# A mixture-of-experts front: statistics taken earlier, another split of the norm, sums before the low half, first tile prepared ahead

## The reference, cut to what matters

```python
x = x + tanh(g_xattn[1]) * L1_xattn(layernorm(x), ctx, mask, ...)
x = x + tanh(g_ffn[1]) * L1_ffn(layernorm(x), ...)

def L1_ffn(hidden, norm_weight, router_w, sw1, sb1, sw2, sb2, ew1, eb1, ew2, eb2):
    var = mean(square(hidden), axis=-1, keepdims=True)
    normed = hidden * rsqrt(var + 1e-08) * norm_weight
    shared = maximum(normed @ sw1 + sb1, 0.0) @ sw2 + sb2
    probs = sigmoid(flat @ router_w.T)              # 8 experts
    scores, idx = top_k(probs, 2)
    w = scores / (sum(scores, axis=-1, keepdims=True) + 1e-06)
    h = maximum(einsum('td,edh->teh', flat, ew1) + eb1[None], 0.0)
    eo = einsum('teh,eho->teo', h, ew2) + eb2[None]
    return shared + einsum('teo,te->to', eo, comb)  # comb holds w at idx
```

## Time and profile before

| | us |
|---|---|
| median of 3 runs | 1716.51 |
| lowest, highest | 1713.88, 1717.43 |
| the profiled execution's own time | 1717.06 |
| its span, from first to last instruction | 1715.3 |
| TensorE busy | 1420.7 (83%) |
| VectorE busy | 1235.3 (72%) |
| ScalarE busy | 1116.1 (65%) |
| GpSimd busy | 214.6 (13%) |
| mean granted TensorE clock | 0.917 |

### The profile page before, as it was taken

How to read it: one execution, slowest core, us unless ns; L and a number is a source line. 1 busy time by engine, 2 the same in 40 slices (tenths; PEclk the granted TensorE clock), 3 DMA queues, 4 the chain that set the end, 5 groups by cost and what they waited for, 6 DMA issues and landing times. The chain is left out here.

```text
span 1715.3 us, 40917 instructions
## 1 busy us (share of the span) xinstructions
PE 1420.7 (83%) x15436; PEld 1010.6 (59%) x15436; DVE 1235.3 (72%) x3086; ACT 1116.1 (65%) x2453; POOL 214.6 (13%) x189
## 2 busy tenths in 40 slices
PE   1799999999999992680638898989889588899996
PEld 1467666766666762440625566566666366678884
DVE  6478888788788777678656898989888675334443
ACT  5467777777777763375236888888888452356663
POOL 4400000001000001200041000000000000034443
PEclk9999999999999997795857999999999588999998
DMA  4123232233222211000021121211100162112221
GB/s 143 52 69 109 83 96 90 81 105 95 97 93 93 72 56 56 1 0 0 1 78 40 49 82 42 82 42 33 33 17 11 32 226 63 47 30 45 48 49 23
DMA packets 64912, 105.72 MB, mean 62 GB/s; under 512 B 7433, under 2 KB 38898, under 8 KB 63570
## 3 DMA queue, kind: packets, MB, share of 16 engines
q1 hardware_dynamic: 58002, 94.83, 17.5%
q0 software_dynamic: 6720, 8.27, 2.9%
HBM read 68.88 MB, written 35.11 MB: 61 GB/s over the span
## 5 line engine op out<-in xcount | busy, mean ns | idle before, releaser
L1272 ACT ACTIVATE a_p<-a_s,a_nb 112x375 f32<-112x375 f32 x256 | 140.9, 598 | 26.2 <-DVE a_nb L1373 25.3
L294 PE MATMUL a_ps_o<-a_vh,a_pt 125*128 125x64 f16 (+1 forms) x1536 | 153.2, 183 | 3.0 <-ACT a_pt L1285 0.8
L1197 PE MATMUL a_ps_t<-ident,a_p 112*128 112x112 f32 x768 | 119.4, 288 | 40.0 <-ACT a_p L1272 39.5
L296 PE MATMUL a_ps_o<-a_vh,a_pt 125*128 125x64 f16 (+1 forms) x1536 | 151.3, 182 | 0.0
L295 PE MATMUL a_ps_o<-a_vl,a_pt 125*128 125x64 f16 (+1 forms) x1536 | 151.2, 182 | 0.0
L584 ACT ACTIVATE a_pt<-a_ps_t 125x336 f16<-125x336 f32 x256 | 102.7, 448 | 68.6 <-PE a_ps_t L515 68.0
L576 ACT ACTIVATE a_p<-a_ps_s,a_nb 112x375 f32<-112x375 f32 x256 | 143.8, 573 | 3.3 <-DVE a_scaled L667 3.3
L294 PEld LDWEIGHTS a_ps_o<-a_vh,a_pt 125*128 125x128 f16 x1536 | 133.8, 98 | 15.7 <-ACT a_pt L1285 7.4
L1364 DVE TENSOR_TENSOR a_s<-a_ps_s,a_mask 112x750 f32<-112x750 f32 x128 | 119.8, 936 | 26.2 <-PE a_ps_s L1187 21.1
L295 PEld LDWEIGHTS a_ps_o<-a_vl,a_pt 125*128 125x128 f16 x1536 | 131.2, 98 | 11.3
L1197 PEld LDWEIGHTS a_ps_t<-ident,a_p 112*128 112x128 f32 x768 | 81.4, 148 | 94.6 <-issue 80.1
(11 more groups left out here) (360 smaller groups left out, 4553.7 us busy)
## 6 DMA issues: line engine op xcount, KB each, us to landing
a_piece<-in_w SPq DMA_DIRECT2D x72, 256.0 KB, 3.1
split_weights<-a_pair SPq DMA_DIRECT2D x72, 256.0 KB, 3.4
w<-split_weights SPq DMA_DIRECT2D x8, 1024.0 KB, 6.1
a_ctx<-in_ctxT SPq DMA_DIRECT2D x16, 375.0 KB, 3.6
ctx<-a_cx SPq DMA_DIRECT2D x16, 375.0 KB, 4.3
a_cx<-ctx SPq DMA_DIRECT2D x16, 375.0 KB, 5.2
w1h<-split_weights SPq DMA_DIRECT2D x2, 1792.0 KB, 14.0
w1l<-split_weights SPq DMA_DIRECT2D x2, 1792.0 KB, 16.6
```

Source lines behind the costliest of these rows:

```text
L294: nc.tensor.matmul(out, wh, mh, start=(i == 0), stop=False)
L296: last = nc.tensor.matmul(out, wl, mh, start=False, stop=(i == n - 1))
L1197: mm = nc.tensor.matmul(ps_t[:, 2 * (g % 2) + i, t * S:(t + 1) * S], p32[:, g % 2, i, t * KV:t * KV + 128], ident32[0:S, 0:S], start=(t == ...
L1272: nc.scalar.activation(p32[:, g % 2, i, 0:NC], s2[:, g % 2, i, :], ACT.Exp, bias=nb[:, g % 2, i:i + 1], scale=-1.0).then_inc(exp_done, 1)
```

## The change

It has four parts.

1. The 16 `bn_stats` leave the front. VectorE issues them in the last slots of the second attention: five in each of the slots 128, 129 and 130, and the last one behind the last `W`. `stats` becomes a buffer that both phases see.
2. VectorE norms the blocks 0 to 11 group by group, with `low_x` of the group before behind each group of norms; the splits of the router's weights and of the biases move behind `low_x(0)`. ScalarE does the square roots first, then norms the blocks 12 to 15, then makes its small copies, and only then `high_x`. TensorE transposes two groups before the first `up`.
3. In a step, VectorE's `add` stands before `low`.
4. The register loads of the expert numbers, the transposition of tile 0 and its split move to the end of the front, in the buffers `tile_xh`, `tile_xl` that both phases see. The routed experts start with the first layer of tile 0.

```diff
@@ attention1_phase, VectorE
                     low(name, b)
                 if 0 <= g - 2 < G and (g - 2) % NP == NP - 1:
                     normalise((g - 2) // NP)
+                if g == G:
+                    dve.wait_ge(job_lo, NUMBER["W", B - 2] + 1)
+                if G <= g < G + 3:
+                    for t in range(5 * (g - G), 5 * (g - G) + 5):
+                        nc.vector.bn_stats(stats[:, t, :], x_res[:, t, :])
+            dve.wait_ge(job_lo, NUMBER["W", B - 1] + 1)
+            nc.vector.bn_stats(stats[:, B - 1, :], x_res[:, B - 1, :])
@@ moe_front_phase, SyncE
-                if g < NG // 2:
+                if g < NG - 1:
                     sp.wait_ge(normed, TG * (g + 1))
                 else:
-                    sp.wait_ge(normed_act, TG * (g + 1 - NG // 2))
+                    sp.wait_ge(normed_act, TG)
@@ moe_front_phase, TensorE
             for g in range(NG):
                 transpose(g)
-                if g < NG - 1:
-                    up(g)
+                if g > 0:
+                    up(g - 1)
             route()
...
                 if n == FIND_AT:
                     find()
+            pe.wait_ge(experts_ready, 1)
+            for n in range(NPACK):
+                experts.append(pe.snap(pe.value_load(tile_expert[0:1, n:n + 1], min_val=0, max_val=8 ** PACK - 1)))
+            pe.wait_ge(xt_in[0], 16)
+            pe.wait_ge(index_ready, 1)
+            for k in range(KD):
+                mm = nc.tensor.transpose(px[:, 0, k * 128:(k + 1) * 128], xt32[:, 0, k * 128:(k + 1) * 128], ident32[:])
+            mm.then_inc(tile_transposed, 1)
@@ moe_front_phase, ScalarE
+            act.wait_ge(var_ready, 1)
+            nc.scalar.activation(small[:, 1, :], small[:, 0, :], ACT.Sqrt).then_inc(std_ready, 1)
+            act.wait_ge(var_ready, 2)
+            nc.scalar.activation(small[:, 4, :], small[:, 3, :], ACT.Sqrt).then_inc(std_ready, 1)
+            act.wait_ge(scale_ready, 1)
+            act.wait_ge(kept, 16 * B)
+            for t in range(B - TG, B):
+                nc.scalar.activation(norm[:, t, 0:D], norm[:, t, 0:D], ACT.Identity, bias=small[:, 7, t:t + 1],
+                                     scale=small[:, 6, t:t + 1]).then_inc(normed_act, 1)
             act.wait_ge(small_in, NSMALL)
...
-            for t in range(HALF, B):
-                nc.scalar.activation(norm[:, t, 0:D], norm[:, t, 0:D], ACT.Identity, bias=small[:, 7, t:t + 1],
-                                     scale=small[:, 6, t:t + 1]).then_inc(normed_act, 1)
-                if t % 4 == 3:
-                    high_x(t // 4 - 2)
+            high_x(0)
+            high_x(1)
+            hidden(0)
             high_x(2)
-            hidden(0)
+            hidden(1)
             high_x(3)
-            hidden(1)
...
+            act.wait_ge(tile_transposed, 1)
+            nc.scalar.activation(xth[:, 0, :], px[:, 0, 0:D], ACT.Copy).then_inc(tile_hi, 1)
@@ moe_front_phase, VectorE
-            for t in range(B):
-                last = nc.vector.bn_stats(stats[:, t, :], norm[:, t, 0:D])
             stat(last)
...
-            for t in range(HALF):
-                nc.vector.tensor_scalar(norm[:, t, 0:D], norm[:, t, 0:D], mv[:, t, 0:1], small[:, 6, t:t + 1],
-                                        ALU.subtract, ALU.mult).then_inc(normed, 1)
-            low_x(0)
-            low_x(1)
+            for g in range(NG - 1):
+                for t in range(g * TG, g * TG + TG):
+                    nc.vector.tensor_scalar(norm[:, t, 0:D], norm[:, t, 0:D], mv[:, t, 0:1], small[:, 6, t:t + 1],
+                                            ALU.subtract, ALU.mult).then_inc(normed, 1)
+                if g > 0:
+                    low_x(g - 1)
+                if g == 1:
+                    dve.wait_ge(nw_ready, 1)
+                    dve.wait_ge(rw_hi, KD)
...
+                    dve.wait_ge(b2_hi, 1)
+                    nc.vector.scalar_tensor_tensor(out=b2[:, 1], in0=b2_32, scalar=WS, in1=b2[:, 0], op0=ALU.mult,
+                                                   op1=ALU.subtract).then_inc(b2_ready, 1)
...
             for n in range(10, STEPS + LAG + 1):
+                if n % HC1 == LAG and n > LAG:
+                    add(n // HC1 - 1)
                 if n < STEPS:
                     low(n)
-                if n % HC1 == LAG and n > LAG:
-                    add(n // HC1 - 1)
...
+            dve.wait_ge(tile_hi, 1)
+            nc.vector.tensor_tensor(xtl[:, 0, :], px[:, 0, 0:D], xth[:, 0, :], ALU.subtract).then_inc(tile_lo, 1)
@@ routed_experts_phase
-            experts = [pe.snap(pe.value_load(tile_expert[0:1, n:n + 1], min_val=0, max_val=8 ** PACK - 1))
-                       for n in range(NPACK)]
...
             expert(0)
-            transpose(0)
...
-            split_x(0)
```

More of the change, by code:

```diff
@@ L1467, in moe_front_phase @@
          rows_out, numbered, shared_in, w1_in, up_done, relu_done,
-         h_hi, h_lo, down_done, bias_chain, added, gate_made) = (sem(f"m_{n}") for n in names)
+         h_hi, h_lo, down_done, bias_chain, added, gate_made, experts_ready) = (sem(f"m_{n}") for n in names)
         y_in = [sem(f"m_y_in{i}") for i in range(2)]
+        experts, xth, xtl, tile_transposed, tile_hi, tile_lo = first_tile
         NSMALL = 16 * 4
@@ L1767, in _ @@
             nc.vector.tensor_scalar(var, mv[:, :, 1], 1e-5, None, ALU.add).then_inc(var_ready, 1)
-            dve.wait_ge(nw_ready, 1)
-            dve.wait_ge(rw_hi, KD)
-            for k in range(KD):
-                last = nc.vector.scalar_tensor_tensor(out=rw[:, k, 1, :], in0=rw32[:, k, :], scalar=nws[:, k:k + 1],
-                                                      in1=rw[:, k, 0, :], op0=ALU.mult, op1=ALU.subtract)
-            last.then_inc(rw_ready, 1)
             reciprocal_root(var, std, rstd, 1)
@@ L1940, in routed_experts_phase @@
         y, half = sb("e_y", [128, YR, D]), sb("e_half", [128, 2, D])
+        p2 = ps("e_p2", [128, 2, 512])
+        p1 = ps("e_p1", [128, 4, 512])
         px = ps("e_px", [128, 2, 512])
-        p1 = ps("e_p1", [128, 4, 512])
-        p2 = ps("e_p2", [128, 2, 512])
-        names = ("x_transposed", "x_hi", "x_lo", "up_done", "relu_done", "h_hi", "h_lo", "down_done", "half_ready",
-                 "y_ready", "y_out")
-        (x_transposed, x_hi, x_lo, up_done, relu_done, h_hi, h_lo, down_done, half_ready, y_ready,
-         y_out) = (sem(f"e_{n}") for n in names)
+        experts, xth, xtl, x_transposed, x_hi, x_lo = first_tile
+        names = ("up_done", "relu_done", "h_hi", "h_lo", "down_done", "half_ready", "y_ready", "y_out")
+        (up_done, relu_done, h_hi, h_lo, down_done, half_ready, y_ready, y_out) = (sem(f"e_{n}") for n in names)
         block = ctx.enter_context(nc.Block())
@@ L2108, in _, with moe_phase @@
                                              ).then_inc(y_out, 16)
-def moe_phase(nc, A, x_all, xh, xl, ident32, tanh_g, rows, out, kept, split_w, w2, w2s, w2_in):
+def moe_phase(nc, A, x_all, xh, xl, ident32, tanh_g, rows, out, kept, split_w, w2, w2s, w2_in, stats):
     with ExitStack() as ctx:
@@ L2121, in moe_phase @@
         xt_in = [sem(f"tile_x_in{i}") for i in range(XR)]
+        xth, xtl = sb("tile_xh", [128, 2, D], F16), sb("tile_xl", [128, 2, D], F16)
+        first_tile = ([], xth, xtl, *(sem(f"tile_{n}") for n in ("x_transposed", "x_hi", "x_lo")))
         w1 = [[sb(f"w1{part}{k}", [128, E, FF1], F16) for k in range(KD)] for part in ("h", "l")]
         moe_front_phase(nc, A, x_all, xh, xl, ident32, tanh_g, split_w, w1, w2s, w2_in, tile_expert, tile_b1, pick, share,
[L2124 to L2125 removed]
+                        target, xt32, xt_in, rows, out, kept, y, stored, stats, first_tile)
+        routed_experts_phase(nc, w1, w2, tile_expert, tile_b1, pick, share, target, xt32, xt_in, rows, out, stored, ident32,
+                             first_tile)
 def program(nc, A, out):
```

43 lines of the change are left out of this document (18 added, 25 removed).

## The result

The changed kernel takes 1688.73 us (median of 4 runs, 1686.98 to 1696.70) against 1715.71 us before (4 runs, 1713.88 to 1717.43). The medians differ by 27.0 us, where 23 were forecast; the ratio over all runs is 0.9849 with a 95% interval of 0.9826 to 0.9872. The profiled execution took 1688.88 us. Two later series of the same kernel on other occasions gave 1691.30 and 1690.86 us (ratios 0.9847 and 0.9856), so 25 to 27 us is the size of the gain.

A forecast was written before the change was run, and what follows sets the result against it. TensorE was taken as the bound in experts and steps, with stalls and 1.2 GHz stretches in the front. 5.3 - 0.4 + 0.6 + 2.6 + 6.8 + 3.5 + 4.6 = 23.0 us gave 1693.5 us, range 1688.5 to 1702.

The forecast's parts named there:

- Statistics: Sixteen bn_stats leave VectorE's path in the front for its idle time in the attention's tail: 5.3 us gained, 0.4 cost.
- Chain of scales: Biases' split and its wait leave VectorE's path between the two square roots, with ScalarE's table load hidden: 0.6 us gained.
- Ramp: From VectorE's first norm to the router's products, 14.9 us becomes 12.3: 2.6 us gained, bounds +4 to 0.
- the ramp gives nothing: Rival: before the router's products, ScalarE becomes what is waited for and the clock rises late: 1696.1 us, chance 0.10.
- Sums first: In the 32 steps, TensorE's three waits on the groups' sums nearly vanish: 6.8 us gained, bounds 5 and 7.5.
- Clock: TensorE's stretches at 1.2 GHz in the front's steps shrink as the waits go: 3.5 us gained, between 0 and 6.
- the slow clock stays: Rival: stalls go, but 1.2 GHz stretches come as often, in bias products and after the router's: 1697.0 us, chance 0.22.
- First tile: From the front's last product to tile 0's first up, register loads start early, beside the last matmuls: 4.6 us gained.
- loads wait for the array: Rival: at the front's end, register loads wait until TensorE's array is empty, 2.4 us later: 1695.9 us, chance 0.18.
- no effect: Rival: steps do not wait on the sums; loads and statistics take as long elsewhere: 1714 us, chance 0.03.
- slower: Rival: TensorE stays at 1.2 GHz for all of the front's steps: 1773 us, chance 0.02.

The follow-up runs named there:

- statistics in the front: The changed kernel with the 16 bn_stats moved back from the attention into the front: 1695.60 us, ratio 0.9877.
- old ramp: The changed kernel with the norm split and the orders of TensorE, ScalarE, VectorE and SyncE as before, statistics still in the attention: 1698.19 us, ratio 0.9886.

## Why the prediction was right

The time lies in the range, 4.8 us below the value forecast in the first series and 2.2 and 2.6 in the later ones. In the first series it is only 0.2 us above the range's low end (1688.5). That the steps forecast are the ones that gained is shown below; but up to 4.4 us of the first result are the draw ahead of W, which the forecast did not know of, and it was luck that this did not carry the time out of the range. Step by step:

- **Statistics**, 5.3 - 0.4: mis-sized. The statistics themselves are gone from the path at a cost of 0.1, not 0.4, and that ahead of W. But 1.2 us of idleness and long instructions that they had covered come up (0.32 + 0.47 + 0.37), so they gave 4.1, as the kernel that puts them back shows by itself, and TensorE stands still for 10.56 us and not for 9.7. What I missed is that the statistics had covered something behind the block's start.
- **Chain of scales**, 0.6: measured 0.56. That the table load is hidden was right. What I did not see is that the order of ScalarE is worth 2.8 to 3.3 us on top: I priced it at nothing, since before it was hidden by the statistics, and it would have been the next to be late.
- **Ramp**, 2.6: measured 2.66, with the router's products 12.26 us behind the first norm (12.3 forecast), one slow `up` as forecast, and the clock rising 7.2 us behind T (7.4 forecast). So the rival that the ramp gives nothing falls for this stretch. The right size rests on a draw, though, and is in part luck: with the new order T to R took 15.1 to 16.9 us by the point at which the clock rises and falls, and of the 2.66 us the router gave back 1.05 in the first profile, at the low clock. That term was missing.
- **Sums first**, 6.8: 7.2 by the waits. The first group waits 0.3 as forecast.
- **Clock**, 3.5 between 0 and 6: 5.4, near the upper bound. The rival that the slow clock stays falls for the steps (12.4 us come with the sums' order alone, in both directions); my doubt, a stretch at the bias products, was seen in one profile of twelve. Its other half, a slow stretch after the router's small products, held: it is there in all twelve, for 3.4 or 6.8 us.
- **First tile**, 4.6: 5.5. The loads did start while the array worked, 2.4 us before its end, and the first load took 488 ns instead of 1421, 0.9 of the 1.1 us that I had put at the bound. The rival that loads wait for the array falls.
- Sum by the profile: 4.6 + 2.7 - 1.1 + 12.4 + 5.5 = 24.1 us for 23.0. The clock's term, the tile's and the sums' were too small by 1.9, 0.9 and 0.4, the statistics' too large by 0.8, and the router's 1.1 was missing; that leaves 24.3, within 0.2 of the measured. So the sum came within 1.1 us in part because errors of 3.2 us one way and 1.9 us the other cancel.
- The rivals *no effect* and *slower* are out, by the steps' 91.5 us, with no slow stretch behind the first step.

## What to carry to other kernels

When work leaves a path, list what ran beside it: here 5.3 us of statistics had hidden a wait for DMA with a table load (2.8 to 3.3 us) and 1.2 us at the block's start, and only the first was moved along with it. An engine that is the bound can lose more than its wait: here the slow clock that came with three waits of 2.5 us cost 5.4 us more. So put the short work that it waits for first in the step. And before a small gain is believed or chased, compare the same stretch in several profiles: the draw ahead of the change was as large as most of its terms.

## What the runs showed of the hardware

- VectorE's first TENSOR_SCALAR of the block ends 4.83 or 4.84 us behind W in all eleven profiles that have no statistics in the front, with the memsets ahead of it (nine) and without (two). The second ends 6.40 or 6.41 us behind W in the nine of them in which it does not wait for a late root. Taking away 0.6 us of work there gained 0.00 us. A TENSOR_SCALAR of 0.17 us then shows 0.64 or 1.12.
- TensorE's clock rises at no fixed distance from its work. After a stillness of 10 to 15 us it rose 3.4 us behind the first transposes (statistics in the front), 6.3 (before) and 9.1 (old ramp). In the first of these only 16 transposes in f32 had run since 14.65 us of idleness, and the first `up` was already at 2.4 GHz:

```profile
1374.37 3.25 PE L1570 MATMUL m_p<-ident,x_res 112*128 112x112 f32 x16 [14.65 <-DVE x_res L1790]
1377.72 0.37 PE L294 MATMUL m_p<-xh,w1h 128*128 128x448 f16 x1
```

  The Trainium skill ("TensorE: Matmul & The Clock Gate", Part 4: PE-mode transpose) says that transposes do not count as busy for the clock. This row speaks against it: nothing else had run.
- The three profiles with the new ramp and T to R of 15.1 to 15.2 us are the three that were slow at 1326 us, and the eight with 16.6 to 16.9 were not (the old ramps left aside). The slow stretch at the router lasts 3.4 us in those three and 6.8 us in the eight. The draw ahead of W is thus partly given back behind it. Why is open.
- A register load right behind a block's start takes 1.4 us, in a running stream 0.3 to 0.5 (but the third of five took 1.1 in both kernels that spread them over the steps). Loads run while the array still works: here from 1470.2, with the last product ending at 1472.6.
